# A two-layer kernel with two routed layers: the second layer's routing split by sequences

## The reference, cut to what matters

```python
# layer 0: x (2 sequences, 1024 tokens, 128), 16 heads of 8, causal attention
s = attention(layernorm(x)) @ WO                   # added in the finish below
w = softmax(top2(h @ gate)); y = sum_e w_e * (silu(h @ w1[e]) * (h @ w3[e])) @ w2[e]   # 8 experts, I=512
# layer 1: W_omega, cumulative sums, cos/sin: a recurrence over 1024 positions
omega = h @ W_omega.T ; phi = cumsum(omega * scale / sqrt(pos)) ; ...
ctx = concat(cm_real, cm_imag, ret_real, ret_imag) ; a = gelu(layernorm(ctx) @ W1.T) @ W2.T
# layer 1, experts: groups of 256 tokens (G=8), E=8 experts, capacity C=64 slots
raw = softmax(logits); idx1 = argmax(raw); idx2 = argmax(rest)
p1 = cumsum(m1) - m1 ; keep where p1 < C
p2 = cumsum(m2) - m2 + count(m1) ; keep where p2 < C
# each kept token goes to slot p of its expert; expert: (gelu(x w0) * (x w1)) wo, H=688
```

## Time and profile before

| | |
|---|---|
| median of three timed runs | 658.17 us |
| the profiled execution: time, span | 658.66 us, 656.9 us |
| mean granted clock of PE | 0.964 |
| busy PE, DVE, ACT, POOL | 91%, 75%, 50%, 25% |
| chain that ended last: PE | 11%, then DVE 1% |

### The profile page before, as it was taken

The page is one execution under the profiler, slowest core; times in us unless marked ns, Lnnn a source line. Parts: engine busy times, 40 slices in busy tenths (PEclk is TensorE's granted clock), DMA queues, the critical chain, the costliest instruction groups (busy, mean ns, idle before and its releaser), DMA issues. The chain is left out here.

```text
span 656.9 us, 12382 instructions
## 1 busy us (share of the span) xinstructions
PE 594.7 (91%) x4214; PEld 365.6 (56%) x4215; DVE 490.1 (75%) x1169; ACT 325.3 (50%) x581; POOL 163.5 (25%) x146
## 2 busy tenths in 40 slices
PE   1878999999999999899999998949989799999996
PEld 0523644444453545899999843426446355555654
DVE  7799889999988898455555598246898288987455
ACT  1752367575766766555555467721323352254134
POOL 2000000000143441133333300000068668843200
PEclk9877799999999999999999999987999899999999
DMA  8980606060713181211111070061012114320232
GB/s 191 239 281 22 219 16 185 19 201 3 204 38 100 36 224 25 49 49 45 48 48 40 25 197 2 2 197 61 1 44 66 22 47 120 109 81 17 69 76 64
DMA packets 53692, 57.18 MB, mean 87 GB/s; under 512 B 8651, under 2 KB 37355, under 8 KB 53595
## 3 DMA queue, kind: packets, MB, share of 16 engines
q1 hardware_dynamic: 49310, 49.73, 27.1%
q0 software_dynamic: 4320, 6.81, 3.2%
q10 hardware_dynamic: 12, 0.01, 0.0%
HBM read 42.19 MB, written 18.85 MB: 93 GB/s over the span
## 5 line engine op out<-in xcount | busy, mean ns | idle before, releaser
L692 ACT ACTIVATE arena<-banks 128x512 f32<-128x512 f32 (+1 forms) x304 | 156.2, 586 | 100.3 <-PE banks L1588 57.9
L1602 PE MATMUL banks<-arena 96*128 96x512 bf16 (+3 forms) x384 | 120.4, 343 | 5.2 <-DVE mpart L1082 2.8
L1585 PE MATMUL banks<-arena 128*128 128x512 bf16 (+3 forms) x384 | 116.8, 331 | 6.5 <-ACT arena L692 2.8
L1085 DVE TENSOR_REDUCE mpart<-banks 128x1 f32<-128x512 f32 x128 | 85.8, 684 | 9.0 <-PE banks L1602 8.4
L1082 DVE CUSTOM_DVE_ANT_0 banks<-banks,arena 128x512 f32<-128x512 f32 (+1 forms) x128 | 78.9, 636 | 9.6 <-PE banks L1602 6.6
L1523 PE MATMUL banks<-arena 128*128 128x128 f32 x624 | 76.3, 275 | 1.0 <-ACT arena L642 1.0
L1523 PEld LDWEIGHTS banks<-arena 128*128 128x128 f32 x624 | 72.8, 192 | 1.5 <-ACT arena L642 1.5
L1644 PE MATMUL banks<-arena 128*9 128x512 f32 (+3 forms) x768 | 70.8, 487 | 0.0
L733 ACT ACTIVATE arena<-banks 125x512 f32<-125x512 f32 (+2 forms) x48 | 28.5, 595 | 81.0 <-PE banks L1757 57.0
L1585 PEld LDWEIGHTS banks<-arena 128*128 128x128 bf16 x384 | 38.0, 100 | 53.9 <-issue 26.0
L543 POOL DMA_INDIRECT slots<-rows_a,posn x16 | 15.5, 967 | 194.6 <-PE banks L1585 185.0
(11 more groups left out here) (289 smaller groups left out, 901.9 us busy)
## 6 DMA issues: line engine op xcount, KB each, us to landing
k_parts<-arena SPq DMA_DIRECT2D x6, 768.0 KB, 7.8
arena<-in_L_ffn_experts_w_dram SPq DMA_DIRECT2D x2, 2048.0 KB, 10.6
arena<-results SPq DMA_DIRECT2D x8, 512.0 KB, 6.8
arena<-k_parts SPq DMA_DIRECT2D x7, 576.0 KB
arena<-q_parts SPq DMA_DIRECT2D x28, 144.0 KB
arena<-in_L_ffn_w_kernel_dram SPq DMA_DIRECT2D x8, 344.0 KB
slots<-in_pad_rows_dram SPq DMA_DIRECT2D x1, 2535.0 KB, 11.0
arena<-slots SPq DMA_DIRECT2D x39, 65.0 KB
```

Source lines behind the costliest of these rows:

```text
L692: act.activation(Pr[:, r % 4, heads[0]:heads[-1] + 1, 0:n], ring_e[e % 3][:, 0:len(heads) * n].rearrange("p (j c) -> p j c", j=len(heads)) ...
L1085: ins = dve.tensor_reduce(part, ps[:, 0:n], AX_X, ALU.max)
L1585: ins = pe.matmul(ring_e[e % 3][:, at * n:at * n + n], QK[:, slot, j, 1, P * kt:P * kt + P], QK[:, slot, j, 0, q:q + n], start=True, stop= ...
L1602: ins = pe.matmul(ps[:, at * n:at * n + n], QK[0:TALL, slot, j, 0, P * i:P * i + P], QK[0:TALL, slot, j, 1, 512 * half:512 * half + n], st ...
```

## The change

- The second layer's routing is done per sequence. The first sequence's maximum, exponential, choice, places and four one-hot matrices (`oh0`) are steps of `MIDDLE` beside the attention; `places1` takes the sequence as an argument.
- `dispatch(g)` on PE: groups 0 to 2 go ahead of the second sequence's last turned rows, into banks 0 to 2; group 3 behind the logits; groups 4 to 7 behind the second sequence's places. The projections' order is 1, 2, 0, 3.
- The slot numbers (`slot_of`, `destination`) leave the place ahead of the experts and become pieces of `recurrence`.
- The `ones_d` products on W1 (`wg_ps`) go behind expert 1's second step.
- DMAs on SP: `iota` (64 numbers now, in the space of `cmp`) with its own semaphore before the first layer's experts' blocks; `pscale` and `rpos` ahead of the wait for the attention's end; `store_parts(1)` ahead of `load_group(1)`.

```diff
-          28: ..., 45: [("logits1",), ("scale",)]}
+          28: ..., 45: [("logits1",)], 46: [("route_max",)], 49: [("route_exp",), ("scale",)], 50: [("route_choice",)], 56: [("places1",)], 57: [("route_places",)]}
...
             store_parts(0)
+            store_parts(1)
             load_group(1)
-            store_parts(1)
...
+                    sp.wait_ge(Z["blkpos_ready"], 1)
+                    sp.dma_start(iota, bass.AP(pos_rows.tensor, 2 * S, [[0, P], [1, C1]])).then_inc(Z["ld_iota"], 16)
                     first_blocks()
...
+            sp.wait_ge(Z["f_done"], 2)
+            sp.dma_start(pscale, ...)
+            sp.dma_start(rpos, ...)
             sp.wait_ge(Z["pv_done"], NG * NS)
...
+            def dispatched(g):
+                act.wait_ge(Z["disp_ps"], g + 1)
+                ps = banks[:, g, :] if g < G1 // 2 else psM[:, g % 2, :]
+                act.copy(XT1[:, :, g, :], ...).then_inc(Z["disp_sb"], 1)
...
             sqrt_of(1)
+            for g in range(3):
+                dispatched(g)
...
+            route_exp(1)
+            dispatched(3)
+            for g in range(G1 // 2, G1):
+                dispatched(g)
...
+                    elif step[0] == "route_places":
+                        route_places(0, unit_ready(), Z["m_free"])
+                        unit += 1
+                        dve.wait_ge(Z["ld_iota"], 16)
+                        for g in range(G1 // 2):
+                            one_hot(g, oh0[:, 2 * g:2 * g + 2, :])
...
+            route_max(1)
+            route_choice(1)
+            route_places(1, psM[:, 1, :], Z["pre_sb"])
+            for g in range(G1 // 2, G1):
+                one_hot(g, oh[:, 2 * g - 8:2 * g - 6, :])
...
-            for a in range(2):
+            def slot_of(a):
                 picked(r_[2 + a], chosen[a], R[5 + a], R[4])
...
-            for a in range(2):
+            def destination(a):
                 link(dve.tensor_tensor(r_[4], r_[6 + a], r_[2 + a], ALU.subtract))
...
             def recurrence(e, k):
 
-                if (e, k) == (0, 1):
+                if (e, k) == (0, 0):
+                    slot_of(0)
+                elif (e, k) == (1, 0):
+                    destination(0)
+                elif (e, k) == (2, 1):
+                    slot_of(1)
+                    destination(1)
+                elif (e, k) == (0, 1):
                     phase_half(0)
...
+            def dispatch(g):
+                pe.wait_ge(Z["oh_ready"], g + 1)
+                ps, source = (banks[:, g, :], oh0) if g < G1 // 2 else (psM[:, g % 2, :], oh)
+                for i in range(2):
+                    ins = pe.matmul(ps, xn[:, 2 * g + i, :], source[:, (2 * g + i) % 8, :], start=(i == 0), stop=(i == 1))
+                ins.then_inc(Z["disp_ps"], 1)
...
+                    elif step[0] == "places1":
+                        ps = unit_free()
+                        places1(0, ps)
+                        pe.wait_ge(Z["pre_ps"], 2)
+                        pe.sem_inc(Z["m_ready"], 1)
+                        unit += 1
...
+            for g in range(3):
+                dispatch(g)
             for c in range(2, 4):
                 pe.wait_ge(Z["xn1_ready"], c + 1)
...
+            pe.wait_ge(Z["disp_sb"], 3)
...
             ins.then_inc(Z["lg_ps"], 1)
+            dispatch(3)
...
-            for c in (1, 2, 3, 0):
+            for c in (1, 2, 0, 3):
                 if c == 0:
                     pe.wait_ge(Z["lg_sb"], 5)
+                elif c == 3:
+                    pe.wait_ge(Z["disp_sb"], 4)
...
-            places1(psM[:, 1, :])
+            places1(1, psM[:, 1, :])
...
+                    if (e, k) == (1, 1):
+                        pe.wait_ge(Z["wprep"], 1)
+                        for c in range(4):
+                            ins = pe.matmul(psO[:, 512:768], ones_d[:, :], W1g[:, c, :], start=(c == 0), stop=(c == 3))
+                        ins.then_inc(Z["wg_ps"], 1)
```

More of the change, by code:

```diff
@@ L313, in build @@
         oh = region(18112, 8 * 512).rearrange("p (n c) -> p n c", n=8)
-        iota = region(25280, 512)
+        oh0 = region(A2 + 8192, 8 * 512).rearrange("p (n c) -> p n c", n=8)
+        iota = cmp[:, 0:C1]
         dest = region(25792, E * 4, I32)
@@ L674, in experts0, with route_exp @@
                 silu(0, NB0 - 1)
+            def route_exp(b):
+                half = rt[:, 1, QT * b:QT * b + QT, :]
+                act.wait_ge(Z["gates_d"], 2 + b)
+                act.activation(half, half, ACT.Exp).then_inc(Z["gates_exp"], 1)
+            def dispatched(g):
+                act.wait_ge(Z["disp_ps"], g + 1)
+                ps = banks[:, g, :] if g < G1 // 2 else psM[:, g % 2, :]
+                act.copy(XT1[:, :, g, :], ps.rearrange("p (e c) -> p e c", e=E)).then_inc(Z["disp_sb"], 1)
             def gate_half(times, c):
@@ L1062, in finish, with halves, route_max @@
                 return dve.tensor_tensor(x1[:, tiles, :], x1[:, tiles, :], ya[:, tiles, :], ALU.add)
+            chosen = [sel_b[:, 0, :, :], sel_b[:, 1, :, :]]
+            def halves(b):
+                tiles = slice(QT * b, QT * b + QT)
+                return [t[:, tiles, :] for t in R], [t[:, tiles] for t in r_], [t[:, tiles, :] for t in chosen]
+            def route_max(b):
+                R, r_, _ = halves(b)
+                link(dve.tensor_reduce(r_[0], R[0], AX_X, ALU.max))
+                dve.tensor_tensor(R[1], R[0], over_experts(r_[0]), ALU.subtract).then_inc(Z["gates_d"], 1)
@@ new lines, in route_places @@
+            def route_places(b, ps, read):
+                R, _, chosen = halves(b)
+                first, second, total = (ps[:, 64 * i:64 * i + 64].rearrange("p (n e) -> p n e", e=E) for i in range(3))
+                dve.wait_ge(Z["pre_ps"], 2 + b)
+                link(dve.tensor_scalar(R[7], total, float(C1), None, ALU.min))
+                dve.scalar_tensor_tensor(R[4], first, 1.0, chosen[0], ALU.add, ALU.mult)
+                dve.tensor_copy(R[5], first)
+                link(dve.tensor_tensor(R[6], second, R[7], ALU.add))
+                dve.sem_inc(read, 1)
+                link(dve.scalar_tensor_tensor(R[10], R[6], 1.0, R[3], ALU.add, ALU.mult))
+                link(dve.tensor_tensor(R[4], R[4], R[10], ALU.add))
@@ L1183, in _ @@
             dve.wait_ge(Z["lg_sb"], 5)
[L1184 to L1212, removed]
+            route_max(1)
[3 more added lines that the diff above has]
+                one_hot(g, oh[:, 2 * g - 8:2 * g - 6, :])
+            dve.wait_ge(Z["ld_L1"], 16 * 6)
             dve.wait_ge(Z["el_done"], 1)
@@ L1469, in counts, with places1 @@
                 pe.matmul(ps[:, 256:256 + n], ones_b, chosen, start=True, stop=True).then_inc(Z["pre_ps"], 1)
[L1471 to L1482, removed]
+            def places1(b, ps):
+                pe.wait_ge(Z["selb_ready"], 2 + b)
+                tiles = sel_b[:, :, QT * b:QT * b + QT, :]
+                odd = ps[:, 0:128].rearrange("p (a g i e) -> p a i g e", a=2, i=2, e=E)
+                total = ps[:, 128:192].rearrange("p (g i e) -> p i g e", i=2, e=E)
+                part = tiles.rearrange("p a (g i) e -> p a i g e", i=2)
+                pe.matmul(ps[:, 0:128].rearrange("p (a m) -> p a m", a=2), before_b, tiles.rearrange("p a n e -> p a (n e)"),
+                          start=True, stop=False)
+                for a in range(2):
+                    pe.matmul(odd[:, a, 1, :, :], ones_b, part[:, a, 0, :, :], start=False, stop=a == 1)
+                pe.matmul(ps[:, 128:192], ones_b, tiles[:, 0, :, :].rearrange("p n e -> p (n e)"), start=True, stop=False)
+                for i in range(2):
+                    ins = pe.matmul(total[:, i, :, :], ones_b, part[:, 0, 1 - i, :, :], start=False, stop=i == 1)
+                ins.then_inc(Z["pre_ps"], 1)
@@ L1728, in _ @@
             ins.then_inc(Z["cb_ps"], 1)
-            for g in range(G1):
-                pe.wait_ge(Z["oh_ready"], g + 1)
-                if g == 1:
+            for g in range(G1 // 2, G1):
+                if g == 5:
                     pe.wait_ge(Z["pre_sb"], 2)
-                if g >= 2:
+                elif g >= 6:
                     pe.wait_ge(Z["disp_sb"], g - 1)
[L1735 to L1741, removed]
+                dispatch(g)
             pe.wait_ge(Z["om_done"], 4)
```

51 lines of the change are left out of this document (33 added, 18 removed).

## The result

The changed kernel took 663.71 us in the median of five runs (661.56 to 665.0), the kernel before 658.17 beside it: a ratio of 1.0082, interval 1.0061 to 1.0104. It is slower by about 5.4 us.

The account below looks back on a forecast made before the run. PE, busy 91% of the span, waits 1.08 us at expert 4 for weights held behind 32 scatters; +2.8 (scatters) - 0.8 (DVE caught up) + 1.8 (restart clock) = +3.8 on 658.17 gives 661.9 us, range 656.5 to 668.

Parts of the forecast that it names:

- The bound: At expert 4, PE's way through the experts meets slot numbers, 32 scatters and weights; the latter ended 1.08 us later.
- The start of the experts: Second layer's expert 0 on PE starts at 467.5 instead of 475.06, 7.6 us earlier; bounds 463.5 and 470.5.
- the clock term: Transposes and logits on PE: a filled hole delays the clock's fall, saving 1.4 us, at most 2.0.
- Slot numbers and scatters: POOL begins scatters at 485.3, 6.1 us later; they take 54 us, the last ending at 539.3, +2.8.
- the slow spell: PE's experts 506.27 to 529.73: 23.5 us between products down instead of 15.4; any repeat goes into expert 4's wait.
- the forecast's ten meetings at 1.3: Scatters meeting long DVE operations up to the end of expert 3: ten at 1.3 us add 13 us.
- List to weights: From the last scatter everything keeps its distance: expert 4's first weights issued 4.3 us ahead of PE's restart, now 545.1.
- PE meanwhile: PE is through expert 3 at about 527, then idle some 18 us; savings in the experts before go into that wait.
- The restart at half clock: Behind the wait at expert 4, PE restarts at 1.2 GHz: +1.8 us (0 to +4).
- The gain of 0.8: Behind expert 4's wait, DVE has caught up, so the 0.8 us that PE twice waited for it go.
- Rival A: Scatters end by 529, before PE asks for expert 4; the 7.6 us gain passes through: 650.6 us; chance 0.15.
- theory S: The experiments' theory: the lengthened list chain sets expert 4's start; added guess: back-to-back scatters stretch PE's spell in expert 2.

Follow-up runs that it names:

- earlier trace: Profiled execution of the kernel before, unchanged: 658.66 us, span 656.9 us.
- Experiment 6: Kernel before with only the slot numbers and destinations moved between the first experts: 668.21 us, ratio 1.0152.
- 1: Changed kernel with slot numbers and destinations of both choices put ahead of the experts again: 651.31 us, ratio 0.9866.
- experiment 2: Changed kernel with the wait for all scatters and the list's reading put behind expert 4's weights: 652.51 us, ratio 0.9904.
- 3: Changed kernel with two scatters instead of 32, other tokens' results not put in place: 643.02 us, ratio 0.9749.
- first trace: Profiled execution of the changed kernel, the longest of its five: 665.0 us, span 663.2 us.
- experiment 8: Changed kernel once more, unchanged, for a second trace: 664.56 us, span 662.8 us.
- 4: Changed kernel with both choices' slot numbers and destinations ahead of the experts and the list read behind expert 4's weights: 646.12 us, ratio 0.9801.
- 10: Changed kernel, slot numbers still between the experts, with the list read behind expert 5's weights: 661.04 us, ratio 1.0055.
- 11: Changed kernel with the first choice's slot numbers and destinations ahead of the experts, the second's inside, list read behind expert 4's weights: 642.17 us, ratio 0.9768.
- both traces of before: The kernel before, profiled unchanged twice: 658.66 us, and once more 657.8 us.
- 5: Kernel before with the scatter wait and the list's reading moved behind expert 4's weights: 649.7 us, ratio 0.9856.
- 7: Changed kernel, slot numbers ahead of the experts, list read behind expert 4's weights, first three dispatches moved behind the second sequence's logits: 654.17 us, ratio 0.9938.

## Why the prediction was right, and where it was not

**The bound: right.** The earlier trace rows show one short wait, and the whole difference passes through it. Experiment 6 gives the sign by itself, 1 to 3 take the loss away in three ways. The forecast of 661.9 (+3.8) stands against 663.7 (+5.5).

**The start of the experts: 467.5 forecast, 470.49 measured.** The attention was 1.4 us later already ahead of any new step; in experiment 8 this was 0.3, so it belongs to the execution. The edits in the attention's tail cost 0.07 where 0.5 was set. The larger part is the clock term: 1.4 us were to be saved because the hole is full. The table by stretches after (columns: length, busy time and count of PE, PEld, DVE, ACT, POOL, then granted clock, DMA share, GB/s), to be held against the earlier trace rows:

```profile
436.00:443.20 7.20, 6.69 (x26) 3.47 (x25) 5.86 (x25) 1.72 (x4) 0.00 (x0) 1.00 0.82 248
444.00:446.00 2.00, 1.20 (x6) 0.80 (x7) 1.64 (x7) 0.39 (x1) 0.00 (x0) 0.74 0.37 106
446.00:454.00 8.00, 8.00 (x25) 5.71 (x24) 3.16 (x15) 2.64 (x5) 0.00 (x0) 0.50 0.08 20
```

The clock did stay at 2.4 GHz through the hole, but fell to 1.2 at about 445, behind the 2.0 us in which PE still waits for DVE, and the transposes and logits ran at half clock all the same: DVE's wait ahead of the logits' copy is 4.42 us, as the 4.44 before. In experiment 2, whose code up to here is the same, the clock fell later, and the term comes out:

```profile
446.29 0.23 DVE L1248 COPY rt<-banks 128x64 f32<-128x64 f32 x1 [2.48 <-PE banks L1784]
```

1.94 us less, the 2.0 that the prediction had as its most. Expert 0 started at 465.78 there, at 467.1 to 467.3 in experiments 1, 4, 10 and 11, and at 468.6 to 470.5 in 3, 8 and the first trace. So the term should have been a range: it came out anywhere from 0 to 1.9, in executions of the same code. In the first trace the logits' copy came 2.4 us late (450.07 against 447.7). From there to the first dispatch it was 10.8 us against 10.3, since dispatch and projections stood in the low clock too (PE late behind the choice by 3.15 at 458.20 instead of 2.3), and from there to expert 0 9.60 against 9.5.

**Slot numbers and scatters: right.** The first scatter was forecast 17.8 us behind expert 0's start and came at 17.9 (488.37 - 470.49); 17.9 in experiments 2, 8 and 10 as well. In experiment 8, free of the spell, POOL's timeline has ten scatters over 1.6 us and no wait above 0.31 us:

```profile
487.30 0.97 POOL L555 DMA_INDIRECT dest<-idt,posn  x1 [17.60 <-DVE posn L1293]
...
495.81 2.94 POOL L555 DMA_INDIRECT dest<-idt,posn  x1 [0.30 <-DVE arena L1411]
...
539.88 0.96 POOL L555 DMA_INDIRECT dest<-idt,posn  x1 [0.30 <-issue]
```

53.5 us in all, 13.2 over the 40.3 of free ones: the forecast's ten meetings at 1.3. In the first trace it is 53.45 too, by another way: the spell took meetings with DVE away and brought waits for the pace instead (1.39 and 2.43 us in the fence above), which are waits for the count of `hid1_done`, put there by the program itself. That both traces come to the same length is luck. The Trainium skill (SBUF — State Buffer, Who interferes with whom), read as the prediction read it, as ten whole operations of DVE added to the scatters, would have given 9 us more; the measured 53.5 goes against that. The reading was also wider than the section, which counts copies, casts and `tensor_scalar` as the 2-port kinds: nine of the ten are other operations, of 2.28 us each (`tensor_tensor`, `scalar_tensor_tensor` and scans).

**List to weights: 4.3 us forecast, 5.3 in the first trace (543.40 to 548.68), 4.1 in experiment 8** (542.77 to 546.84). It accounts for 1.0 of the first trace's miss. What stretched that one transfer stays open.

**PE meanwhile: right only in experiment 8.** Forecast: some 18 us idle, SP's wait over 25. Measured in the first trace: 1.64 and 20.0; in the second: 18.54 and 33.1. By the prediction's own list of signs ("PE runs on into expert 4 within a microsecond or two") the first trace speaks against it; only the second, and experiments 1, 2 and 6, show the mechanism in the open. The sign was badly chosen, since the prediction also said that the slow spell, if it came, would go into that wait. So it did: it took 17 of the 18 us at no cost. The restart at half clock was set at +1.8; in experiment 8 expert 4's first product to its products down takes 551.81 - 546.84 = 4.97 us, in the first trace 552.22 - 548.68 = 3.54: +1.4. In the first trace PE had hardly stood, and that cost was not paid. The gain of 0.8 from DVE having caught up never came. PE's waits between 545 and 600 in the changed kernel are the very ones of the earlier trace rows:

```profile
PE banks L1824 <- DVE arena L1411: 0.8, 2, 0.6
```

They are there after a wait of 18.5 us as well, so no backlog makes them. With the second trace the sum closes: 4.49 (expert 4 at 546.84 against 542.35) + 1.4 = 5.9, which is 662.8 - 656.9. Against the forecast of +3.8 that is +1.9 from the start of the experts, -0.2 from there to the weights, +0.8 for the gain that never came and -0.4 for the restart: the number was close in part because terms offset each other.

**Rival A** had the spell eat the gain at the start and the scatters end before 529; they ended at 541.8. It did name the right lever: with the first scatter at 470 to 472 (experiments 1, 4 and 11, of which 4 and 11 also have the hold moved) the gain at the start passes through.

**What stays open: the slow spell.** In both traces of before, in the first of after and in 10, DVE, ACT and SP wait for PE's signals after PE's rows end. From the end of expert 1's products down by its rows to SP's release it is 4.1 and 6.3 us in before, 11.3 in after and 11.3 in 10. The ends of PE's rows are modelled, so whether the signals were late or the products themselves is not shown. In the first trace of after, PE's products down of expert 1 end by 508, and DVE and SP are let go at the same moment, 519.26 (ACT at 522.08):

```profile
519.26 0.69 DVE L1418 COPY arena<-banks 128x512 f32<-128x512 f32 x1 [11.04 <-remote]
```

```profile
519.26 0.28 SPq L512 DMA_DIRECT2D arena<-in_L_ffn_wo_kernel_dram  x1
```

POOL's scatters run free at 1.26 us during it, in a train of over fifteen. Traces of 1 to 8 and 11, most with 32 scatters as well, have no spell (in 3 there are only two scatters). So a train of scatters is not enough to bring it, which is the guess that was added to theory S, and whether it is needed was not tried. All nine runs of 10 lie between 660.0 and 662.8, so there it seems to come each time; the two traces of the changed kernel differ in it. What decides this is open. In 10 its price shows: 34.6 - 15.4 = 19.2 us in the trace, and 18.9 by the ratios against 11. In before and after it lay under the wait for the list, so it is also unproven that 11 can never have it; its five runs lie within 1.2 us of each other.

## What to carry to other kernels

Where two chains meet in one short wait, price the change on both before counting a gain: the experts started 4.6 us earlier, but the list's chain behind that start had grown by 10 us. Work that only one late consumer needs may be deferred, but the first item that starts a long serial train (here 17.9 us to the first of 32 scatters) belongs ahead of the experts, and only the first half of it. And a DMA queue that holds weights behind an unrelated wait should have that wait put later, as far as its result allows; how far is to be measured (here one expert later gave 9.5 us in the kernel before, and two gave 661.0 in the changed one).

## What the runs showed of the hardware

- By the profile's rows PE's signals reached SP and DVE 4 to 11 us late (519.26 against 508, 515.86 against 511.79), and ACT too, in four of the thirteen traces, always around expert 2. The mean time did not show it where a longer chain lay over it.
- With 5.3 us of dense products in the hole of 7.2 us PE was granted 2.4 GHz all through it (0.68 of full speed before). Behind a wait of 2.0 us the clock fell to 1.2 GHz in the first trace (0.50 from 446 to 454), in experiment 2 only later (1.00 from 444 to 446, 0.54 from 446 to 448), with the same code.
- Two executions of one kernel with waits of PE for the same weights that differ by 17 us (1.64 and 18.54) took the same time within 0.5 us.
- A scatter of 0.96 us that began during a DVE operation of 2.28 us ended about 0.8 us behind it (521.69 to 523.78, DVE until 522.94, in experiment 8); one that had begun before such an operation kept its 0.96 (518.16, the scan from 518.33), and DVE's operations kept their 2.28 in both cases.
